# Layer-2 factorization network: the first 64 batch rows in two parts of 32, with the order planned anew

## The reference

```python
e = emb_table[feat_index]                      # 512 x 39 x 16
flat = e.reshape(512, -1)
h1 = relu(einsum('bhd,bmd,ohm->bod', e, e, conv_w1) + conv_b1[None, :, None])      # 128 outputs
nxt, hi1 = split(h1, 2, axis=1)                # 64 and 64
h2 = relu(einsum('bhd,bmd,ohm->bod', nxt, e, conv_w2) + conv_b2[None, :, None])    # 128 outputs
res = concatenate([hi1, h2], axis=1).sum(axis=2)
y = relu(bn(flat @ deep_w1 + deep_b1))         # 400
y = relu(bn(y @ deep_w2 + deep_b2))            # 400, batch norm over the 512 samples
return concatenate([flat @ linear_w + linear_b, res, y], axis=1) @ out_w + out_b
```

## Time and profile before

| | |
|---|---|
| median of 3 runs | 464.21 us |
| the profiled execution | 464.01 us |
| its span | 462.2 us |
| TensorE (PE) busy | 403.8 us, 87% |
| VectorE (DVE) | 362.8 us, 79% |
| ACT | 198.2 us, 43% |
| POOL (GpSimd) | 319.2 us, 69% |
| DMA, mean over the span | 190 GB/s |

### The profile page before, as it was taken

One profiled execution on the slowest core, in us unless ns is written; L12 is line 12 of the kernel. 1 busy time (PEld: TensorE's weight loads), 2 busy tenths in 40 slices (PEclk: granted clock), 3 DMA queues, 4 the chain that ended last, 5 costly groups with the idle time before them and its releaser, 6 DMA issues. The chain is left out here.

```text
span 462.2 us, 4571 instructions
## 1 busy us (share of the span) xinstructions
PE 403.8 (87%) x1238; PEld 229.4 (50%) x1238; DVE 362.8 (79%) x369; ACT 198.2 (43%) x252; POOL 319.2 (69%) x232
## 2 busy tenths in 40 slices
PE   0001959999999999999999999989999999979996
PEld 0001524554465555556555555546557565655563
DVE  6222658979958888999779777999874988998994
ACT  1104012327432751465156524734564447656443
POOL 5787777775848667886888878832478268729662
PEclk9999988999999999999999999999999999999999
DMA  3756959999998988899999979988957999998910
GB/s 64 146 85 146 152 63 244 238 171 210 221 235 186 226 205 192 191 228 243 237 209 215 219 183 206 232 227 212 220 128 186 236 230 236 241 258 213 237 38 2
DMA packets 41726, 87.95 MB, mean 190 GB/s; under 512 B 15836, under 2 KB 21275, under 8 KB 41700
## 3 DMA queue, kind: packets, MB, share of 16 engines
q1 hardware_dynamic: 28693, 80.48, 70.9%
q0 software_dynamic: 5120, 1.32, 7.9%
q10 hardware_dynamic: 7887, 5.86, 5.4%
HBM read 86.34 MB, written 1.28 MB: 190 GB/s over the span
## 5 line engine op out<-in xcount | busy, mean ns | idle before, releaser
L540 POOL TENSOR_TENSOR zl<-ring,zh 128x1024 fp32r<-128x1024 f32 x60 | 142.5, 2389 | 83.0 <-ACT zh L1022 78.9
L526 POOL DMA_INDIRECT G<-in_emb,idx_all x160 | 161.5, 1010 | 48.2 <-issue 41.7
L662 DVE TENSOR_TENSOR ring<-p_n,ring 128x1024 f32<-128x1024 f32 x147 | 174.0, 1217 | 0.9
L1022 ACT ACTIVATE zh<-ring 128x1024 fp32r<-128x1024 f32 x81 | 85.3, 1056 | 133.3 <-DVE ring L662 130.2
L833 PE MATMUL p_h<-ring,w2s 128*128 128x512 f32 x264 | 124.6, 602 | 6.3 <-DVE ring L662 5.4
L833 PE MATMUL p_n<-placed,w1s 125*128 125x512 f32 (+2 forms) x192 | 92.0, 603 | 0.0
L662 DVE TENSOR_TENSOR placed<-xa,p_x 125x1024 f32<-125x1024 f32 (+2 forms) x45 | 54.7, 1216 | 37.0 <-PE p_x L812 37.0
L833 PEld LDWEIGHTS p_h<-ring,w2s 128*128 128x128 f32 x264 | 50.6, 193 | 56.0 <-issue 44.3
L833 PE MATMUL p_h<-zh,w2l 128*128 128x512 f32 x178 | 68.2, 464 | 1.6 <-DVE zh L625 1.6
L812 PE MATMUL p_x<-stack,put 103*125 103x512 f32 (+3 forms) x116 | 52.5, 534 | 9.7 <-DVE stack L635 9.3
L833 PE MATMUL p_h<-zh,w2h 128*128 128x512 f32 x178 | 56.0, 396 | 0.0
(11 more groups left out here) (113 smaller groups left out, 303.0 us busy)
## 6 DMA issues: line engine op xcount, KB each, us to landing
ring<-xs_scratch SPq DMA_DIRECT2D x294, 256.0 KB, 5.6
xa<-xs_scratch ACTq DMA_DIRECT2D x21, 156.0 KB
G<-in_emb,idx_all POOLq DMA_INDIRECT x160
xs_scratch<-xT ACTq DMA_DIRECT2D x16, 64.0 KB
...
```

Source lines behind the costliest of these rows:

```text
L526: nc.gpsimd.indirect_dma_start(G[:, b % 2, DIM * f:DIM * (f + 1)], None, emb[:, :], bass.IndirectOffsetOnAxis(idx_all[:, b, f:f + 1], 0)). ...
L540: nc.gpsimd.tensor_tensor(low_of(s), z_of(s), high_of(s).bitcast(F32), ALU.subtract).then_inc(s_low_pool, 1)
L662: nc.vector.tensor_tensor(z_of(s), by, x, ALU.mult).then_inc(s_z, 1)
L1022: nc.scalar.activation(high_of(s), z_of(s), ACT.Copy).then_inc(s_zh, 1)
```

## The change

Block 0 becomes two parts of 32 rows (`HALVED = 1`); the other seven blocks stay whole, so there are 9 parts, 9 stages after stage -1, and 234 tiles. Part 0 and 1 have 512 columns, one chunk. Part b's stage in the change corresponds to block b-1's before, from part 2 on. What follows from it, and what else is edited:

- A half part is gathered as 32 rows x 4 field groups, 10 gathers, 2 transposes, 2 copies. The index comes in five DMAs (two of them on ACT's queue), not one. Its rows go to `flatT` not by ACT, but by 6 DMAs per part from the scratch (`load_flat`), issued by SP behind the first ring load of stage 3; all 24 dense loads (`load_deep`), which stood ahead of the scratch write, now stand right behind those.
- `xa` of part 0 is loaded by SP and ACT, that of part 1 by SP at ring load 3 (`FIRST_LOADS`, 5 before).
- The three operations behind part 0's layer 1 are on ACT, not on VectorE; ACT no longer waits for all small loads, only for the biases.
- `out_of_l2` is one operation over all columns, and the next part's first layer-2 matmul waits for all of it.
- `X_AT`, `P_AT`, `DVE_LOW`, `POOL_LOW`, the squares' place, `T_AT`, the places of `high_x` and `low_x` and the dense branch's places are planned anew; 88 tiles are split rather than 89, and VectorE makes the x residue of parts 1, 2, 3, 4 and 7. Gathers of part 2 wait for a product each, one per 700 columns.
- The two pairs of `dw2` loads change places.

```diff
-FLAT_FIELDS = [8, 8, 4]
-FLAT_ROWS = [DIM * n for n in FLAT_FIELDS]
+HALVED = 1
+HALVES = 2 * HALVED
+ROWS_OF = [ROWS // 2] * HALVES + [ROWS] * (BLOCKS - HALVED)
+PARTS = len(ROWS_OF)
+FROM = [sum(ROWS_OF[:b]) for b in range(PARTS)]
+TOK_OF = [DIM * r for r in ROWS_OF]
+CHUNKS_OF = [t // BANK for t in TOK_OF]
+
+
+GROUPS = [128 // r for r in ROWS_OF]
+PER_GROUP = [2 * HALF_F // g for g in GROUPS]
+
+FLAT_FIELDS = [[8, 2] if g == 4 else [8, 8, 4] for g in GROUPS]
...
+X_AT = {0: [5, 7, 8, 14, 17, 20], 1: [6, 7, 9, 14, 15, 20], 2: [3, 8, 9, 15, 16, 18], 3: [0, 2, 4, 8, 12, 13],
+        4: [0, 2, 5, 8, 10, 13], 5: [0, 2, 5, 8, 10, 13], 6: [0, 4, 7, 9, 12, 14], 7: [0, 2, 4, 6, 8, 10], 8: []}
+P_AT = {0: [25], 1: [24], 2: [1, 22, 23], 3: [18, 20, 25], 4: [17, 20, 25], 5: [20, 25], 6: [], 7: [], 8: []}
...
+DVE_LOW = {-1: [], 0: [1, 12, 25], 1: [13, 24], 2: [6, 13, 14, 23, 25], 3: [18, 20, 25], 4: [7, 14, 20, 25],
+           5: [6, 9, 14, 25], 6: [1, 8, 15, 16], 7: [1, 12, 19, 20, 22, 25], 8: [0, 2, 9, 10, 17]}
+POOL_LOW = {-1: [], 0: [19], 1: [10], 2: [5], 3: [1, 3, 7, 11, 16, 21], 4: [1, 3, 11, 16, 21],
+            5: [-1, 1, 3, 11, 16, 19, 24], 6: [3, 5, 11, 13, 17, 19, 21, 22, 23, 24, 25],
...
+SQ_AFTER = 4
+
+
+T_AT = {0: 16, 1: 11, 2: 6, 3: 6, 4: 6, 5: 6, 6: 5}
+T_AHEAD = 4
+
+XA_BEHIND, HIGH_X_BEHIND, LOW_X_BEHIND = (6, 6), (12, 13), (13, 14)
+LOW_X_ON_DVE = [1, 2, 3, 4, 7]
+
+FIRST_GATHER, GATHER_COLUMNS, PACED, GATHER_PLACE, GATHER_TILES = 0, 700, 3, 2, 23
+
+T1_PE, T1_ACT, HIGH_X1_ACT, LOW_X1 = (-1, 1), (-1, 3), (0, 4), (0, 2)
+SQ_ACT_AHEAD, SQ_DVE_AHEAD = 6, 3
...
+FIRST_LOADS = 3
...
+        XS_WRITES = [[(0, 0, 4, 8), (1, 0, 3, 2), (1, 3, 1, 1)] if g == 4 else [(0, 0, 2, 8), (1, 0, 2, 8), (2, 0, 1, 4), (2, 1, 1, 3)]
+                     for g in GROUPS]
+        XS_LANDED = [16 * sum(map(len, XS_WRITES[:b + 1])) for b in range(PARTS)]
+        GATHERED = [16 * sum(PER_GROUP[b % 2:b + 1:2]) for b in range(PARTS)]
+        X_COPIED = [sum(map(len, FLAT_FIELDS[:b + 1])) for b in range(PARTS)]
...
+        XA_ACT = {b: (at[0], at[1] + XA_BEHIND[at[0] < HALVES - 1]) for b, at in T_ACT.items()}
+        HIGH_X_ACT = {b: (at[0], at[1] + HIGH_X_BEHIND[at[0] < HALVES - 1]) for b, at in T_ACT.items()}
+        LOW_X = {b: (at[0], at[1] + LOW_X_BEHIND[at[0] < HALVES - 1]) for b, at in T_ACT.items()}
+        T_PE[1], T_ACT[1], HIGH_X_ACT[1], LOW_X[1] = T1_PE, T1_ACT, HIGH_X1_ACT, LOW_X1
...
-        AT_ONCE = 4
         GATHERS = {}
-        for f in range(AT_ONCE, 2 * HALF_F):
-            GATHERS.setdefault(WHERE[f - AT_ONCE], []).append((2 + f // HALF_F, f % HALF_F))
-        for b in range(4, BLOCKS):
-            for f in range(HALF_F):
-                GATHERS.setdefault((b - 3, 2 + 23 * f // HALF_F), []).append((b, f))
+        AT_ONCE = 8
+        place, ready = FIRST_GATHER, 0
+        for b in range(2, PACED):
+            for f in range(AT_ONCE if b == 2 else 0, PER_GROUP[b]):
+                GATHERS.setdefault(place, []).append((b, f))
+                ready += GATHER_COLUMNS
+                while ready >= TOK_OF[SEQ[place][1]]:
+                    ready -= TOK_OF[SEQ[place][1]]
+                    place += 1
+        for b in range(PACED, PARTS):
+            place = max(place, AT[b - 3, 0] + GATHER_PLACE)
+            for f in range(PER_GROUP[b]):
+                GATHERS.setdefault(place + GATHER_TILES * f // PER_GROUP[b], []).append((b, f))
+            place += GATHER_TILES
...
+        def load_flat(eng, b):
+
+            for c, p, first, fields in FLAT_PIECES:
+                src = bass.AP(xs.tensor, xs_at(b, first), [[ROWS_OF[b], DIM * fields], [1, ROWS_OF[b]]])
+                eng.dma_start(flatT[p:p + DIM * fields, c, FROM[b]:FROM[b] + ROWS_OF[b]], src).then_inc(s_flat, 16)
+
+        def load_half_indices(eng, block, g):
+
+            r, n = ROWS_OF[0], PER_GROUP[0]
+            half, quarter = divmod(g, 2)
+            src = idx[ROWS * half:ROWS * (half + 1), block, n * quarter:n * (quarter + 1)].rearrange("(c r) f -> r c f", c=2)
+            eng.dma_start(idx_raw[r * g:r * (g + 1), block, :].rearrange("r (c f) -> r c f", c=2), src).then_inc(s_idx, 16)
...
+            own_wait(sp, s_x, X_COPIED[0])
+            scratch_write(sp, 0, XS_WRITES[0][1:])
+            own_wait(sp, s_xs, XS_LANDED[0])
             sp.wait_ge(s_zero, 4)
-            for dst, src in ((lb_sb[HID_K:, :], lin_b), (ow_y_sb[HID_K:, HID_T - 1:], ow_lin),
-                             (ow_y_sb[0:HID_K, :], ow_y), (ow_h2_sb[:, :], ow_h2), (ob_sb[:, :], ob)):
-                sp.dma_start(dst, src).then_inc(s_small, 16)
-            sp.dma_start(ow_hi_sb[NEXT:128, :], ow_hi).then_inc(s_small, 16)
-
-            own_wait(sp, s_x, len(FLAT_ROWS))
-            scratch_write(sp, 0, XS_PARTS[2:])
-            own_wait(sp, s_xs, XS_LANDED)
-            load_x(sp, 0)
+            load_first_x(sp, 0)
...
+                if m == FIRST_LOADS:
+                    own_wait(sp, s_xs, XS_LANDED[1])
+                    load_first_x(sp, 1)
+                    load_xa(sp, 1)
...
-                if m == FIRST_LOADS:
-                    own_wait(sp, s_xs, 2 * XS_LANDED)
                 for half in range(2):
-                    sp.dma_start(ring[NEXT * half:NEXT * (half + 1), m % RING, :],
-                                 xs_rows(j * FIELDS + min(2 * t + half, FIELDS - 1), NEXT, 0)).then_inc(s_load[m % RING], 16)
+                    sp.dma_start(ring[NEXT * half:NEXT * (half + 1), m % RING, 0:TOK_OF[j]],
+                                 xs_rows(j, min(2 * t + half, FIELDS - 1), NEXT, 0)).then_inc(s_load[m % RING], 16)
+                if j == HALVES + 1 and LOADED[m - 1] < L2_OF[j][0]:
+                    for b in range(HALVES):
+                        load_flat(sp, b)
+                    load_deep()
...
+                    if b < PACED:
+
+                        own_wait(pool, s_z, s + 1)
                     if f == 0:
                         own_wait(pool, s_tp, b - 1)
-                    if b == 2:
-
-                        own_wait(pool, s_z, s + 1)
                     gather(b, f)
...
-            def out_of_first_l1():
-
-                dve.wait_ge(s_small, SMALL)
-                dve.wait_ge(s_mm, LAST_X[0] + 1)
...
+                    if first and b:
+                        pe.wait_ge(s_h2, b)
 
                 def mm(c, w, x, start=False, stop=False):
-                    if start and layer == 2 and b:
-
-                        pe.wait_ge(s_h2, CHUNKS * (b - 1) + c + 1)
...
+                if b >= HALVES:
+                    rows = slice(FROM[b], FROM[b] + ROWS)
+                    for q in range(2):
+                        nc.scalar.activation(flatT[:, 2 * q:2 * q + 2, rows],
+                                             room_of_t(b)[:, 128 * q:128 * (q + 1)].rearrange("p (a b) -> p a b", a=2), ACT.Copy)
+                    nc.scalar.activation(flatT[0:64, 4, rows], room_of_t(b)[0:64, 256:256 + ROWS], ACT.Copy)
+                    nc.scalar.activation(flatT[64:FLAT_TILES[4], 4, rows], room_of_t(b)[0:FLAT_TILES[4] - 64, 256 + ROWS:256 + 2 * ROWS],
+                                         ACT.Copy).then_inc(s_te, 1)
...
-                for c in range(CHUNKS):
-                    nc.scalar.activation(h2s[:, BANK * c:BANK * (c + 1)], p_h2[:, BANK * c:BANK * (c + 1)], ACT.Relu,
-                                         bias=b2_sb[:, :]).then_inc(s_h2, 1)
+                nc.scalar.activation(h2s[:, 0:TOK_OF[b]], p_h2[:, 0:TOK_OF[b]], ACT.Relu, bias=b2_sb[:, :]).then_inc(s_h2, 1)
...
+            own_wait(sc, s_xs, XS_LANDED[0])
+            load_xa(nc.scalar, 0)
...
+            works = [((-1, 5), lambda: (sc.wait_ge(s_bias, 16 * 4), hi_out_of_l1(0), second_n(0), first_n(0)))]
```

336 lines of the change are left out of this document (170 added, 166 removed).

## The result

Over 17 runs of each, side by side, the changed kernel took 462.65 us at the median (458.2 to 465.1), the kernel before 464.84 (463.15 to 465.63): a ratio of 0.995, 95% interval 0.9937 to 0.9962. It is faster by 2.2 us, not by 7.5; 456.5 was forecast and 461.0 was the upper end. The profiled execution took 463.32 us for a span of 461.5.

A forecast was written before the change was run, and what follows sets the result against it. The kernel was taken as a late start, then a solid block of TensorE matmuls and a short tail. An earlier start gives 14.5 us, gathers and deductions leave 7.5: 464.0 - 7.5 = 456.5 us, range 452.5 to 461.0.

The forecast's parts named there:

- Term 3: Half stages to part 4's transposes: TensorE, early, waits for gathers 60 and 80; the 14.5 us lead shrinks to 7.5.
- Term 1: Start of the first part: ten gathers, smaller scratch and x split; first placement at 32.4 us against 43.65.
- rival E: Start: the first part waits for the weights, not for ten gathers; counted in Term 1, no chance given.
- Term 2: Layer 1 in 10.3 us, VectorE's chain in 3.1: layer 2 begins at 45.8, not 67.8, 14.5 us ahead.
- what costs nothing: Stages after part 4's transposes, flat copies and ring loads: extra work is covered; VectorE's ring waits under 1 us.
- the price of a packet: Ring loads on the DMA queues: a 2 KB packet costs 0.12 us, between bounds of 0.10 and 0.216.
- rival D: Half-tile ring loads: a 2 KB packet costs as much as a 4 KB one; 13 us more, 469.5; chance 0.08.
- Rival C: Half stages held by more than gathers: SP's issues, slow clock or late DMA row; 459 to 463.5; chance 0.20.
- its slow clock: Half stages, part of Rival C: the wait for gather 60 brings the slow clock once more, 2.5 us.
- SP's row of 36 DMAs: Flat copies and deep loads before stage 3's ring loads: fits by 2 us; in Rival C late by 3 to 5.
- B: Half stages: gathers hold less, at 1.25 us each; lead of 9.9 us, 454.1; chance 0.15.
- The later stages: From part 4's transposes on: stages run as the kernel before's, moved by one, with VectorE's extra 1.6 us covered.

The follow-up runs named there:

- as_is: The changed kernel, unaltered, run again beside the kernel before: 463.9 us against 464.38, ratio 0.9985.
- split_and_pool_2: Changed kernel with part 2's x residue earlier in VectorE's order and tiles (0,19), (1,10) not split, so no POOL low parts there: 465.63 us, ratio 1.0008.
- after_ring_2: Changed kernel with nearly all ring loads cut to 16 of their 64 partitions (layer-2 sums wrong): 457.58 us against 465.19, ratio 0.9842.

## Why the prediction was wrong

**Direction right, size wrong.** 2.2 us came where 7.5 were forecast, less than anywhere in the range. In the profile the miss stands before part 4's transposes: they were done at 124.7 for a forecast of 115.5, 9.2 us late, and from there on the kernel was 2.2 us quicker than I had allowed. The step that failed is Term 3's path of TensorE through the half stages, where the hand-overs and the wait for ring loads were priced too low or at nothing.

**Term 1 held**: 31.4 for 32.4. ACT did stand behind the weights, until 24.5 (24.9 forecast), so the ten gathers were not the limit (rival E), and reading back took 2.1 us, not 2.9. The first placement came 12 us sooner. **Term 2 held** in its end, 45.77 for 45.8, by some luck: layer 1 took 11.35 us for a forecast of 10.3, and the first placement's 1.0 us to the good paid for it. The lead of 14.5 us was there.

**Term 3 failed**, the gathers' toll. The gathers did run as counted (gather 60 issued at 83.37 for a forecast of 83.5), but they weren't what TensorE met at part 3. "TensorE alone would be there at 84.2" was the bad number: it was there at 93.9. I had priced the wait for the residue at 1.9 and one spell of the slow clock; 3.2 came, with 1.5 for POOL's low part, 0.9 for the tail, 1.0 for a product before part 2's transposes and a second spell of clock 0.50 behind them. With that spell, some 3 us for 6 us at half speed, these account for about 7 of the 9.7 us; the rest lies in gaps that I can't assign. In as_is the same residue was waited for by 2.3 us, the clock stayed at 1.00 in 80 to 88, and part 3 was transposed at 90.91 rather than 93.88; there the clock had fallen at 60 to 66 instead (0.72). At part 4, gather 80 was late by POOL's wait for tile (1,10), in which I had costed the low part (1.35) but not its wait (5.25).

**The ring loads failed too, under "what costs nothing".** "VectorE waits for ring loads by less than 1 us" was said of a kernel that runs ahead with a ring half as deep in columns, on queues that were at 91.7% already late in the kernel before. The wait became 9.6 us, 2.0 of them before the residue that TensorE waited for. With the bytes cut the change gives 457.6, one us from the forecast; but its profile is still 7 us late at part 4's transposes (122.4 for 115.5), so that this nearness is in part luck, helped by late stages that were quicker than allowed. I had looked at the price of a packet, for rival D, and that price was right: in 60 to 92, nearly all half tiles, the queue of the changed kernel shows

```profile
q1 hardware_dynamic: 2886, 4.73, 54.3%
```

that is 0.543 x 16 x 32 = 278 queue-us for 2886 packets of 1.6 KB on average, 0.096 us each and 59 per MB (0.12 for 2 KB, the price that I had taken), where the earlier trace rows gave 66. D, a 2 KB packet as dear as one of 4 KB, is refuted. The Trainium skill, "DMA: Bandwidth & Descriptors", section "Bandwidth", has the rate fall with the size of a transfer, in a table for transfers issued from GpSimd; for SP's loads, from 256 to 128 KB, this trace doesn't show it. What I didn't ask is whether 66 per MB leaves room for a lead. In 118 to 142, and in 142 to 166, the changed kernel reads, and then its queue of ring loads in 118 to 142:

```profile
118.00:142.00 24.00, 22.52 (x64) 11.40 (x63) 20.84 (x19) 7.37 (x13) 14.65 (x13) 1.00 1.05 240
142.00:166.00 24.00, 24.00 (x72) 13.29 (x71) 21.48 (x19) 10.26 (x10) 9.29 (x8) 1.00 0.88 172
```

```profile
q1 hardware_dynamic: 1622, 5.29, 93.6%
```

The last is 359 queue-us for 5.29 MB, 68 per MB.

A stage with 17 loaded tiles of 0.52 MB moves 8.9 MB of ring loads, and x and scratch 0.7 more: 9.6 MB at 68 queue-us each are 653, or 41 us on 16 engines, in a stage that TensorE does in 45.6. By this estimate four or five us of slack per stage, less the gathers, must take every burst. In the changed kernel they sufficed here (47.6 us from part 4's transposes to part 5's, as with the loads cut); in split_and_pool_2, 5.8 us earlier, they did not (52.9).

**Rival C** (more than gathers hold the half stages, 459 to 463.5, chance 0.20) has the result in it, and its slow clock came true. Its other parts did not decide: SP's row of 36 DMAs passed (TensorE has 24.00 busy of 24 from 142 to 166), and SP's issues were the same in number in after_ring_2, which had no ring wait, but shorter too (414 ns for 589), so issuing isn't excluded as a part of it. From 45 to 92 SP spent some 34 of 47 us issuing ring loads. **B** is refuted in its time and its sign: part 4 did wait for gathers, though for POOL's wait and not for their pace. **The later stages** were kinder than taken: from part 4's transposes done to the end I allowed 339, the changed kernel took 461.5 - 124.7 = 336.8.
